# The last mixture of a four-layer kernel, worked off in two batches of tokens with units of 32 rows

## The reference, cut to what matters

```python
def _route_dense(z, k, tau):
    topi = jax.lax.top_k(z, k)[1]
    topv = jnp.take_along_axis(z, topi, axis=1)
    w = jax.nn.softmax(topv / (tau + EPS), axis=1)
    dw = jnp.zeros((N, L), z.dtype)
    return dw.at[jnp.arange(N)[:, None], topi].add(w)
...
x_addr = x_flat @ P_w.T
dw1 = _route_dense(x_addr @ U1.T, K, TAU)      # 3 of 12 experts for the first map
dw2 = _route_dense(x_addr @ U2.T, K, TAU)      # 3 of 12 for the second
dw3 = _route_dense(x_addr @ U3.T, K, TAU)      # 3 of 12 for the bias
h = _apply_mixture(x_flat, dw1, W1)            # sum_e dw1[n,e] * (W1[e] @ x[n]), 256 -> 1024
h = jax.nn.gelu(h, approximate=False)
y = _apply_mixture(h, dw2, W2)                 # 1024 -> 256
y = y + dw3 @ b2
...
x = x + _L1_ffn_ref(_layernorm(x, axis=-1), ...)
```

## Time and profile before

| what | value |
|---|---|
| median of three runs | 1134.04 us (1131.06 to 1135.93) |
| the profiled execution | 1135.87 us, span 1133.7 us |
| PE busy | 1061.7 us, 94% |
| DVE busy | 565.3 us, 50% |
| ACT busy | 409.2 us, 36% |
| POOL busy | 360.9 us, 32% |
| mean granted PE clock | 0.978 |
| moved by DMA | 187.61 MB, mean 165 GB/s |

### The profile page before, as it was taken

How to read it: one execution, slowest core, us unless ns; L and a number is a source line. 1 busy time by engine, 2 the same in 40 slices (tenths; PEclk the granted TensorE clock), 3 DMA queues, 4 the chain that set the end, 5 groups by cost and what they waited for, 6 DMA issues and landing times. The chain is left out here.

```text
span 1133.7 us, 19091 instructions
## 1 busy us (share of the span) xinstructions
PE 1061.7 (94%) x6025; PEld 775.9 (68%) x6025; DVE 565.3 (50%) x1159; ACT 409.2 (36%) x803; POOL 360.9 (32%) x401
## 2 busy tenths in 40 slices
PE   7999999998999999999998999989989888999995
PEld 3788844687999887788763544333357667887873
DVE  3988857765444544677689624043332222111114
ACT  0666644422112131556423444322324333323420
POOL 1221100000111001111103444164437776777760
PEclk8999999999999999999998999999979999999998
DMA  7000050000797001920022555797978998866758
GB/s 223 2 1 0 1 184 1 1 1 2 259 351 238 10 0 38 378 93 0 1 83 74 199 195 186 251 358 253 373 269 295 296 307 286 274 202 210 235 187 304
DMA packets 92417, 187.61 MB, mean 165 GB/s; under 512 B 13821, under 2 KB 34287, under 8 KB 92348
## 3 DMA queue, kind: packets, MB, share of 16 engines
q1 hardware_dynamic: 64482, 109.97, 28.0%
q0 software_dynamic: 22416, 69.75, 19.1%
q10 hardware_dynamic: 5450, 6.95, 1.8%
HBM read 136.57 MB, written 52.17 MB: 166 GB/s over the span
## 5 line engine op out<-in xcount | busy, mean ns | idle before, releaser
L2176 PE MATMUL f_psY<-W,a_W 128*128 x768 | 186.1, 386 | 5.6 <-issue 2.2
L2122 PE MATMUL f_psH<-W,f_xTk 128*128 x384 | 178.6, 604 | 2.3 <-ACT shared L2232 1.8
L2176 PEld LDWEIGHTS f_psY<-W,a_W 128*128 128x128 f32 x768 | 139.8, 192 | 26.4 <-issue 11.1
L2122 PEld LDWEIGHTS f_psH<-W,f_xTk 128*128 128x128 f32 x384 | 69.4, 194 | 77.9 <-issue 77.8
L1736 POOL DMA_INDIRECT W<-p_d,f_rows x96 | 93.9, 978 | 73.2 <-issue 24.4
L2232 ACT ACTIVATE shared<-f_psH 128x512 f32<-128x512 f32 x108 | 64.5, 597 | 140.1 <-PE f_psH L2122 103.6
L2237 ACT ACTIVATE a_W<-f_psV 128x512 f32<-128x512 f32 x108 | 64.5, 597 | 114.8 <-PE f_psV L2154 112.8
L1736 POOL DMA_INDIRECT shared<-h_d,f_half_toks x82 | 80.5, 982 | 48.5 <-issue 24.9
L2352 DVE TENSOR_SCALAR a_W<-W,f_wt 128x512 f32<-128x512 f32 x32 | 16.4, 511 | 157.8 <-DMA W<-p_d,f_rows 103.3
L1517 POOL DMA_DIRECT2D m_eos<-m_eo x32 | 16.8, 526 | 201.8 <-DVE m_eo L1414 200.6
L1736 POOL DMA_INDIRECT a_W<-xn_d,f_toks x54 | 52.4, 970 | 88.4 <-PE f_psT L2105 53.0
(11 more groups left out here) (324 smaller groups left out, 1994.7 us busy)
## 6 DMA issues: line engine op xcount, KB each, us to landing
p_d<-shared SPq DMA_DIRECT2D x108, 256.0 KB, 3.8
W<-in_f_W1T SPq DMA_DIRECT2D x24, 512.0 KB, 9.6
W<-in_f_W2T SPq DMA_DIRECT2D x24, 512.0 KB, 6.2
m_wg<-in_m_Wg SPq DMA_DIRECT2D x16, 512.0 KB, 4.3
m_wu<-in_m_Wu SPq DMA_DIRECT2D x16, 512.0 KB, 5.7
m_wd<-in_m_Wd SPq DMA_DIRECT2D x16, 512.0 KB, 6.2
h_d<-a_W SPq DMA_DIRECT2D x32, 256.0 KB, 5.0
f_stage<-in_f_W2T SPq DMA_DIRECT2D x12, 512.0 KB, 5.3
```

What stands on the lines that cost most here:

```text
L2122: mm = pe.matmul(psH[:, n % 2, :], xTk[:, i, k, :], W1[c][:, e, k, :], start=k == 0, stop=k == KD - 1)
L2176: mm = pe.matmul(psY[:, n % 2, 0:D], hT[:, m % 2, k, :], W2[c][:, e, k, :], start=begin_sum, stop=end_sum)
```

## The change: two batches of tokens, three kinds of tile

The 2048 tokens are two batches of 1024, and each batch gets lists, tiles and memory of its own. The unit is now 32 rows. A batch has 27 tiles: 18 plain, 6 of two units of 64 rows (halves), and 3 of four units of 32 rows (quarters). That is 54 tiles again, of which 36 are plain, 12 are halves and 6 are quarters. A half tile issues each product twice, a quarter tile four times, each for its share of the output partitions. The weights of all but the first unit are copied by DVE into a ring of 12 buffers of 512 columns, for the first and for the second products: a map's weights are four steps of 512 columns, so a half tile needs 4 copies and a quarter tile 12.

- **Routing ahead of the first products** is done for batch 0 alone; batch 1 is routed beside the first products.
- **First products** go tile by tile over the full hidden width. The order is batch 0 plain, batch 0 mixed, batch 1 mixed, batch 1 plain. The 18 mixed tiles stand in one row.
- **Sums**: those of batch 0 run from tile 31 on, beside batch 1's first products, those of batch 1 from tile 8 on beside the second products.
- **Second products** go tile by tile with whole rows gathered: 12 plain tiles of batch 0, then the mixed tiles with plain ones between. The bias products stand behind tiles 2 to 17. The results are added up in PSUM over the full width, so the addition on DVE is gone.
- **Second weights**: experts 0 and 1 are loaded late in the first products, 2 to 9 once all first products are done, 10 behind the first sum of batch 1, and 11 behind the second. DVE waits for all twelve before it copies weights for the first mixed tile of the second products.
- **Tail**: batch 0's results are loaded and added beside the last second products; only batch 1's eight token tiles are left behind them.
- 4 MB of memory that was written once before the first gathers is no longer written.

The core of the diff:

```diff
-PLAIN = B * N * TOP // P
-LT = -(-((B * N * TOP + E1 * (HALF - 1)) // HALF) // 2)
+QUARTER = P // 4
+TB = -(-((N * TOP + E1 * (QUARTER - 1)) // QUARTER) // 4)
+HALVES, QUARTERS = E1 // 2, E1 // 4
+PLAIN = TB - HALVES - QUARTERS
+LT = B * TB
...
+                    out = [(0, i) for i in [*range(PLAIN), *mixed]] + [(1, i) for i in [*mixed, *range(PLAIN)]]
...
+                    out = [(0, i) for i in range(PLAIN - HALVES)]
+                    for j, i in enumerate(mixed):
+                        out.append((0, i))
+                        if j < HALVES:
+                            out.append((0, PLAIN - HALVES + j))
+                    for j, i in enumerate(mixed):
+                        out += [(1, j), (1, i)]
+                    out += [(1, i) for i in range(MIX, PLAIN)]
...
+                                for c in range(2):
+                                    wait(pe, po_ready, 2 * (n - 2) + c + 1)
+                                    for k in range(KD):
+                                        s = KD * c + k
+                                        if m > 1:
+                                            pe.wait_ge(stage_ready, staged(False, n, s, m - 1) + 1)
+                                        for q in range(m):
+                                            at = slice(q * P // m, (q + 1) * P // m)
+                                            weights = W1[:, e, k, c * HH:(c + 1) * HH] if q == 0 else \
+                                                stage[:, staged(False, n, s, q) % STAGES, :]
+                                            mm = pe.matmul(psH[at, n % 2, c, :], xTk[n % 2][:, k, at], weights,
+                                                           start=k == 0, stop=k == KD - 1)
...
+                            def stage_second(n):
...
+                                e = [dve.value_load(owner_of(1, b, i, q), min_val=0, max_val=E1 - 1) for q in range(1, groups(i))]
+                                dve.wait_ge(w2_ld, 16 * E1)
+                                for s in range(STEPS):
+                                    for q in range(1, groups(i)):
...
+                                        dve.tensor_copy(stage[:, j % STAGES, :], W2_steps[:, e[q - 1], s, :]
+                                                        ).then_inc(stage_ready, 1)
...
+                            sp.wait_ge(h_mm, 2 * LT)
+                            for e in range(2, E1 - 2):
+                                load_w2(e)
+                            for u in range(NT, TT):
+                                store_sum(u)
+                                if u - NT < 2:
+                                    load_w2(E1 - 2 + u - NT)
+                            results_stored(sp, 0)
```

More of the change, by code:

```diff
@@ L76 @@
 BIG = 3.0e38
-Turn = namedtuple("Turn", "kind tile seat use free half")
+Use = namedtuple("Use", "second slot step group")
 def wait(eng, sem, value):
@@ L1586, in top3_mixture @@
[L1586 to L1591, removed]
-                    return v.unsqueeze(2).to_broadcast([P, n, E1])
-                def pick(dve, one, r, h, lo, hi):
-                    n = hi - lo
-                    z, eq, least = Z[:, r, lo:hi], tmp[:, 0, lo:hi], first[:, lo:hi]
+                uniti = sb(st, "f_uniti", [P, 3, E1], I32)
@@ L1779, in top3_mixture @@
-                mixed_turns = [u for u in turns if u.tile >= PLAIN]
-                assert [(u.kind, u.tile) for u in mixed_turns] == [("whole", PLAIN + j) for j in range(MIXED)]
-                def owner_of(r, i, h):
-                    n = i if i < PLAIN else PLAIN + 2 * (i - PLAIN) + h
-                    return owner[0:1, r, n:n + 1]
-                def landed(n, slot, ring):
-                    return 16 * len([i for i in range(n) if i % ring == slot])
+                        one.step(dve.tensor_tensor(pair[:, :], pair[:, :], own[:, 0:TB], ALU.add))
@@ new lines, in found_tokens, with first_order @@
+                        one.step(dve.tensor_copy(pairi[:, :], pair[:, :]))
+                        one.step(dve.tensor_copy(dest[:, at], pairi[:, :]))
+                mixed = []
+                for j in range(QUARTERS):
+                    mixed += [PLAIN + 2 * j, PLAIN + 2 * j + 1, PLAIN + HALVES + j]
+                MIX = len(mixed)
+                def first_order():
+                    out = [(0, i) for i in [*range(PLAIN), *mixed]] + [(1, i) for i in [*mixed, *range(PLAIN)]]
+                    assert sorted(out) == [(b, i) for b in range(B) for i in range(TB)]
+                    return out
@@ L2044, in all_sums @@
+                            def all_sums(b):
                                 for s in range(2):
-                                    pool.wait_ge(hs_stored[s], landed((c + 1) * TT, s, 2))
+                                    pool.wait_ge(hs_stored[s], landed((b + 1) * NT, s, 2))
                             def hidden(n):
-                                u = turns[n]
-                                wait(pool, hT_mm, u.free)
-                                if u.kind == "first" and u.tile == QUAD:
-                                    pool.wait_ge(b_mm, TT)
@@ L2273, in _ @@
+                            load_results(act, range(NT + 1, TT, 2))
+                            for i in range(NT, TT):
                                 act.wait_ge(o_ready, i + 1)
@@ new lines, in _ @@
+                            dve.wait_ge(z_copied, 1)
+                            pick(dve, one, 0, 0, 1)
+                            choose(dve, one, 1)
+                            dve.sem_inc(chosen_ready, 1)
+                            dve.wait_ge(count_mm, 2)
+                            lists(dve, one, psN, 1)
+                            for i in range(NT):
+                                match(0, i)
+                            dve.wait_ge(at_used, 2 * NT)
+                            found_tokens(dve, one, 0, 1, psF)
```

1203 lines of the change are left out of this document (608 added, 595 removed).

## The result

Measured side by side, the changed kernel takes 1147.1 us (1144.1 to 1147.9, four runs) and the kernel before 1132.6 (1131.0 to 1135.9): a ratio of 1.0121, 95% interval 1.0099 to 1.0144. It is slower by 14.6 us, where 6 were forecast. The profiled execution took 1144.1 with a span of 1142.2.

The account below looks back on a forecast made before the run. Bounds taken by stretch: DVE in routing, PE in first products, POOL in second. Terms −9.7 + 22.9 − 10.7 + 13.5 − 9.6 = +6.4 gave 1140 us against the median, 8-in-10 range 1106 to 1168.

Parts of the forecast that it names:

- the case forecast: Whole kernel: slower, 1140 us against the median, own range 1125 to 1156, chance 0.44.
- Routing: Ahead of the first products: batch 1's pick and four double matches leave the chain, −9.7 us.
- First products: First products' stretch: 219.7 to 242.6 us, +22.9, as DVE's copies and routing hold up the mixed tiles.
- PE's own need: First products without waits for DVE: 211.6 us, 8.1 less than before.
- DVE's deficit: First products' 18 mixed tiles: DVE's list takes 102 us, PE's 76, so PE waits 26; ends 10 and 41.
- the clock: First products: PE's clock lost after the stalls costs 2 us.
- Quarter tiles: Both maps: four products of 32 rows run nearly free, +6 us together, 3 in each map.
- Gap: Between last first product and first second product: 12.2 to 1.5 us, −10.7, since gathers are issued earlier.
- Second products: Second products' stretch: 259.8 to 273.3 us, +13.5, with a 19.3 us wait for weights at tile 12.
- Tail: After the second products: half the token tiles loaded back, half the issues and adding, −9.6 us.
- DMA: Rival, tiles 34 to 53 of the first products: DMA traffic costs some 13 us more, 1153; chance 0.16.
- One cover alone holds: Rival: 1118 us if only the second products' weights are in time, 1112 if only DVE keeps up; chance 0.18.

Follow-up runs that it names:

- long condition: Sets of runs that took longer throughout: the kernel before 1185 to 1189 us, the changed kernel 1162.
- e3: Changed kernel with the first products' 30 owner loads left out, all 120 copies reading expert 0: 1145.0 us, 17.5 less than the changed kernel.
- e6: Changed kernel with batch 0's copies in the second products reading expert 0 and waiting for its load alone: 1156.1 us, 6.3 less.
- e2: Changed kernel without the first products' copies, owner loads and PE's waits for them: 1126.7 us, 35.7 less.
- the best variant: Changed kernel plus own-expert waits, alternating mixed tiles, earlier owner loads, ACT making fourth-unit copies, and later mixed tiles with earlier sums: 1111.6 us, 0.9813 of the kernel before.

## Why the prediction was right, and where its sizes were off

The direction and the case forecast came out: slower, because DVE's list is longer than PE's in the mixed tiles, and the mixed tile of the second products comes ahead of its weights. The sum was +6.4; the profiled execution shows +8.2 and the median +14.6. Some of the closeness is luck: several terms below are off in ways that cancel, and in the long condition, which the prediction didn't know of, the same change is 2.0% faster.

*Routing*, −9.7: −11.4, the first product at 600.2 instead of near 602.

*First products*, 242.6: 247.8. PE's own need was put at 211.6; without the copies it is 211.7. DVE's deficit was put at 26: 24.9. The term that failed in size is the clock, put at 2: 247.8 − 211.7 − 24.9 leaves 11.2 (short waits for ACT are in both stages, 2.7 and 2.8), and the steps of PE behind its waits add up to some 10 us above 0.43 each. Of the eight waits five (2.0 to 5.8 us) were followed by three to six steps of 0.85; the three others, of 0.5, 1.7 and 3.25 us, were not, so a stall doesn't always cost more than its length. Inside the 26, two errors cancelled. The copies cost 0.35 each and not 0.38, and the owner loads were under-priced: 0.25 each, 7.5, where DVE is idle 14.1 us before the copies and e3 gives 15.7 us of stage time for them.

*Quarter tiles*, 6 in both maps: nothing, by the four products started together; in the second products a quarter tile takes 4.52 us and a half tile 4.53. The span model of the Trainium skill, "TensorE: Matmul & The Clock Gate", section Part 3: Packing small matmuls, is borne out here, where four products start within 0.012 us at the full clock. The estimate of 1.3 worked out from its table, whose row of four is for row tiles, is not.

*Gap*, −10.7: −9.4.

*Second products*, 273.3: 273.5, which is luck, since the errors cancel. A bias product costs 0.77 a tile (5.10 against 4.33), 12.3 for sixteen and not 9.0; the working was also wrong, since it took 0.86 for a step of 512 columns, which is 0.43 at the full clock here and in the prediction's own quarter tiles. A mixed tile costs 0.29 (0.20, and 0.09 in the plain tile behind it), as predicted. The ten loads took 71.8 for 77, 7.2 each, but began only 3.7 after the last first product, when the load ahead of them had landed; PE began 2.8 after it, which the prediction had left out of the wait, and was at the 13th tile 60.0 later for 57.7. The wait was 13.6 for 19.3. The clock cost some 4 for 2.2. What was missed is 5.4 us of further waits for copies, 5.1 of them at two quarter tiles: the prediction had DVE's 120 copies "spread over 33 tiles", but a quarter tile with its loads and a sum in front holds DVE for some 11 us (4.3 + 3.0 + 3.4), where a tile of PE is 4.4 to 5.2. POOL's 132 gathers and scatters at 1.25 us were put at 165 us and were busy for 133 (126 instructions, 1.06 each).

The prediction also took the wait at that tile to be DVE's, for all twelve experts. e6 shows that 8.7 of 14.6 us are there without DVE's wait.

*Tail*, −9.6: −12.5. In the chain the last transfer back shows as 4.17 us where the earlier trace rows had 13.00 and half of it was expected:

```profile
1127.72 4.17 DMA W<-p_d
```

*The rivals.* DMA: the 18 plain tiles from 781 to 848 ran at a share of 0.98 and 371 GB/s, more than the 321 from which the rival was argued, and PE was busy 64.8 of 67. The rival's 13 us were not there. One cover alone holds: e2 is that case made by hand for the copies, −35.7 where the rival was priced at −28; the clock, priced at 2 and measured at some 10, is about the difference. That neither wait is a law of the change is shown by the best variant, with the same split and 35 us less.

## What to carry to other kernels

When one engine feeds another with copies, add up its whole ordered list over the stretch, not its share of the span, and count small loads of indices as full operations: thirty of them were worth 15.7 us here. A stall of PE can cost more than its length: the clock was low behind five of the eight here, and added some 10 us to 24.9. A tile that needs an arbitrary expert belongs behind those that need known early ones: waiting for each expert alone gave 4.2 us, and moving the tile two places, with the sums earlier, another 6.4 on top of the other edits. And a store in a queue behind loads that wait for each other holds up whoever needs its buffer.

## What the runs showed of the hardware that was not expected

- 30 index loads on VectorE's queue, 0.3 us each at the median, held it idle by 1.2 to 2.9 us for three in a row (2.0 to 3.0 at the first three such tiles of the second products), and were worth 15.7 us of stage time.
- Four products of 32 output rows start within 0.01 us at the full clock and step at 0.43, as one of 128.
- A bias product of 256 columns on 32 rows of the array costs 0.77 us between full tiles.
- TensorE's clock fell to its lower level around or shortly behind waits of 4.0, 3.0, 2.0, 4.6 and 5.8 us in the first products, and not behind one of 3.25.
- For sets of runs the same kernel took 1187 us instead of 1132 (before) and 1162 instead of 1147 (after), and the sign of the change turned from 1.3% slower to 2.0% faster.
